# One VectorE instruction of 1024 columns in place of two of 512 in the running sum of the probabilities

## What is computed

```
q, k, v = (z @ w_qkv.T) split into 8 heads of 32
scores  = einsum("bhnd,bhmd->bhnm", q, k) / sqrt(32)
attn    = softmax(scores, axis=-1)
sa      = einsum("bhnm,bhmd->bhnd", attn, v)
out     = sa @ w_agg.T + b_agg
```

## Time and profile before

| | us |
|---|---|
| median of 3 executions | 1822.64 |
| lowest, highest | 1817.12, 1822.80 |
| span of the profiled execution | 1855.2 |
| PE busy | 1449.7 (78%) |
| DVE busy | 1112.1 (60%) |
| ACT busy | 883.7 (48%) |
| POOL busy | 575.7 (31%) |
| first exp of batch 0, last exp of batch 7 | 131.8, 1532.4 |

### The profile page before, as it was taken

The page is one execution under the profiler, slowest core; times in us unless marked ns, Lnnn a source line. Parts: engine busy times, 40 slices in busy tenths (PEclk is TensorE's granted clock), DMA queues, the critical chain, the costliest instruction groups (busy, mean ns, idle before and its releaser), DMA issues. The chain is left out here.

```text
span 1855.2 us, 28644 instructions
## 1 busy us (share of the span) xinstructions
PE 1449.7 (78%) x10308; PEld 902.9 (49%) x10308; DVE 1112.1 (60%) x2276; ACT 883.7 (48%) x1281; POOL 575.7 (31%) x1142
## 2 busy tenths in 40 slices
PE   5669998989698969996999699969998995213565
PEld 3435655555455536554655465536555554112444
DVE  3226765666476747564667476657665884764553
ACT  2235564656465636564656466646565772000111
POOL 1303410452035203520352035204520221035664
PEclk7788998999899989998999899989999997557777
DMA  2152015101610161005300630053004303012221
GB/s 73 36 120 63 1 40 134 56 1 37 143 51 1 29 144 58 1 6 141 85 1 1 138 92 1 1 127 102 2 1 108 99 2 98 0 44 81 90 89 60
DMA packets 73757, 109.47 MB, mean 59 GB/s; under 512 B 12410, under 2 KB 56443, under 8 KB 73595
## 3 DMA queue, kind: packets, MB, share of 16 engines
q1 hardware_dynamic: 66409, 90.47, 19.6%
q0 software_dynamic: 6144, 16.79, 2.8%
q10 hardware_dynamic: 1042, 0.01, 0.0%
HBM read 20.98 MB, written 25.43 MB: 25 GB/s over the span
## 5 line engine op out<-in xcount | busy, mean ns | idle before, releaser
L843 ACT ACTIVATE probs<-scores 128x1024 f32<-128x1024 f32 x512 | 519.3, 1023 | 265.0 <-PE scores L622 171.7
L622 PE MATMUL scores<-query_stack,key_stack 128*128 128x256 f32 x2048 | 410.5, 325 | 110.4 <-issue 86.0
L1062 DVE TENSOR_TENSOR prob_sum<-prob_sum,probs 128x512 f32<-128x512 f32 x640 | 454.8, 759 | 16.2 <-ACT probs L843 16.2
L622 PEld LDWEIGHTS scores<-query_stack,key_stack 128*128 128x128 f32 x2048 | 294.8, 196 | 256.8 <-issue 188.0
L640 PE MATMUL acc<-probs,v_sb 128*32 128x256 f32 x4096 | 331.0, 396 | 8.8 <-ACT probs L843 8.8
L862 POOL TENSOR_TENSOR attn_T<-acc_sb 128x256 f32<-128x256 f32 x64 | 61.9, 966 | 645.8 <-DVE acc_sb L1047 634.2
L663 PE MATMUL shared<-w_sb,chan 128*128 128x512 f32 (+1 forms) x512 | 188.6, 504 | 5.0 <-DVE chan L974 5.0
L1047 DVE RECIPROCAL acc_sb<-acc_sb 128x256 f32<-128x256 f32 x64 | 111.6, 1744 | 107.6 <-ACT acc_sb L833 107.6
L1182 PE MATMUL y_ps<-w_sb,zT 128*128 128x256 f32 x256 | 90.1, 488 | 76.8 <-DVE result L1341 51.4
L1351 ACT ACTIVATE zT<-zT_ps 128x256 f32<-128x256 f32 x64 | 24.6, 384 | 257.4 <-PE zT_ps L1173 209.3
L640 PEld LDWEIGHTS acc<-probs,v_sb 128*32 128x32 f32 x4096 | 88.4, 109 | 111.6 <-issue 43.0
(11 more groups left out here) (164 smaller groups left out, 2046.4 us busy)
## 6 DMA issues: line engine op xcount, KB each, us to landing
query_stack<-hi SPq DMA_DIRECT2D x128, 128.0 KB, 2.5
key_stack<-hi SPq DMA_DIRECT2D x128, 128.0 KB, 2.6
x_sb<-in_x_dram SPq DMA_DIRECT2D x8, 1024.0 KB, 8.2
key_stack<-lo SPq DMA_DIRECT2D x64, 128.0 KB, 2.5
query_stack<-lo SPq DMA_DIRECT2D x64, 128.0 KB, 2.5
v_sb<-v_next SPq DMA_DIRECT2D x16, 512.0 KB, 3.7
out_dram<-resid SPq DMA_DIRECT2D x16, 512.0 KB, 3.3
tokens_scratch<-resid SPq DMA_DIRECT2D x16, 512.0 KB, 4.2
```

Source lines behind the costliest of these rows:

```text
L622: last = pe.matmul(score_ps[u % 2][:, QB * r:QB * (r + 1)], key_stack[:, HG * g + r, P * kt:P * (kt + 1)], query_stack[:, HG * g + r, QB * ...
L843: act.activation(probs[:, u % 3, :], score_ps[u % 2][:, :], ACT.Exp, scale=DH ** -0.5) \
L1062: dve.tensor_tensor(total[:, part], probs[:, (u - 1) % 3, part] if kt == 1 else total[:, part], probs[:, u % 3, part], ALU.add).then_inc(s ...
```

## The change

The loop over the two halves goes. One `tensor_tensor` adds all 1024 columns, it counts the semaphore `summed` up by 1, and the three waits on that semaphore (of the next add, of TensorE's `total` and of ScalarE's exp) count adds and not halves. Nothing changes place.

```
-                    pe.wait_ge(s["summed"], 2 * added * (blk + 1))
+                    pe.wait_ge(s["summed"], added * (blk + 1))
...
-                        act.wait_ge(s["summed"], 2 * (added * ((u - 3) // T) + min(max((u - 3) % T, 1), added)))
+                        act.wait_ge(s["summed"], added * ((u - 3) // T) + min(max((u - 3) % T, 1), added))
...
-                for h in range(2):
-                    part = slice(BANK * h, BANK * (h + 1))
-                    if kt > 1:
-
-                        dve.wait_ge(s["summed"], 2 * (added * (u // T) + kt - 2) + h + 1)
-                    dve.tensor_tensor(total[:, part], probs[:, (u - 1) % 3, part] if kt == 1 else total[:, part],
-                                      probs[:, u % 3, part], ALU.add).then_inc(s["summed"], 1)
+                if kt > 1:
+
+                    dve.wait_ge(s["summed"], added * (u // T) + kt - 1)
+                dve.tensor_tensor(total, probs[:, (u - 1) % 3, :] if kt == 1 else total, probs[:, u % 3, :],
+                                  ALU.add).then_inc(s["summed"], 1)
```

## The result

The changed kernel takes 1864.8 us (median of 4 runs, 1864.3 to 1867.1) against 1822.7 us (4 runs, 1817.1 to 1831.9) for the kernel before: a ratio of 1.0218, with a 95% interval of 1.0191 to 1.0246. It is 42 us slower, 3 us above the upper end of the stated range (1816 to 1862) and 14 above the 1830 to 1851 that the forecast counted as its own. From the first to the last exp of each of the eight batches, added up, it went from 1295.8 to 1337.1 us, +41.3, which is nearly the whole result; the seven boundaries between batches have 104.8 and 106.0 us. Batch 2, by its exps, went from 170.5 to 177.8.

The account below looks back on a forecast made before the run. TensorE's queue was taken to bound the kernel nearly everywhere; changed waits (+15 us) and slow clock (+5) made +20 us on the profiled span, carried to the 1822.6 us median: 1843 us, range 1816 to 1862.

Parts of the forecast that it names:

- The instruction: VectorE's add: 1.21 us for 1024 columns; 0.07 us gained per add where another instruction follows freely, 0.04 lost between dependent adds.
- Rival 4: An add costs 1.37 us, more than its slope says: +0.8 x 7 = +6 us, within the forecast's range, no separate chance.
- GpSimd falls behind: Beside back-to-back adds, one GpSimd operation passes per VectorE instruction: once per 1.2 us with whole adds, per 0.6 with halves.
- Rival 1: GpSimd does not fall behind: the two +1.6 us go to zero, the gains stand, 1816 us; chance 0.17.
- Head scaling: TensorE's 3.4 us wait for GpSimd's head scaling grows by 1.6 us per loop batch, to 5.0; batch 0 by 1.07.
- Store chain: GpSimd chain ahead of the layer-norm rows (0.5 us TensorE wait at 534.4): ends later, +1.6 us in each of six batches.
- Rival 2: Only one of the two places with +1.6 us moves, the other has unseen slack: 1828 us; chance 0.20.
- Exp at 615.4: TensorE's 2.3 us wait for an exp behind a GpSimd chain that meets single adds: +0.2 us per loop batch.
- The gains: Shorter waits: line 922 -0.6 us, batch end -0.1, line 957 -0.07, an exp in batch 0 -0.6, batch 7 -0.8 net.
- The sum without the clock: All changes in waits: 15.6 us over six loop batches, +0.4 in batch 0, -0.8 in batch 7, together +15 us.
- The clock: TensorE at half clock after longer waits: 1.7 us lost at three of 13 places, +5 us; bounds -6 and +22.
- Rival 3: The clock falls behind every longer wait: 15 + 22 = +37 us, 1860 us; chance 0.13.

Follow-up runs that it names:

- the two filled kernels: Changed kernel and kernel before, each with idle 128x512 matmuls put ahead of TensorE's long waits: 1851.5 us (ratio 0.9984) and 1833.8 us (ratio 0.9901).

## Why the forecast was right in its mechanism and short in its sum

**What bounds the kernel.** Right. The time followed TensorE's waits and clock, and 56 us off VectorE's busy time (1112.1 to 1055.8) bought nothing.

**The instruction.** Right: an add that nothing holds up takes 1.22 us (the row at 537.19), forecast 1.21 (the terms as printed, 0.68 + 2 x 0.26, give 1.20), and two dependent ones span 2.49 to 2.50, which is twice that and a gap of 0.05 or 0.06, forecast 0.03. The mean of 1.255 us holds the hold-ups by GpSimd. Rival 4 (1.37) is out. The formula that the forecast took from the Trainium skill, "VectorE: DVE Perf Modes", gives 1.22 for it, and the trace agrees. The saving of 61 us that the same formula gave is close to the 59 of busy time, but by luck: as said above, most of the 59 is standing behind GpSimd that went away.

**GpSimd falls behind.** Right, and the term that decides. Rival 1 fell with the rows of 1.2 us on four columns. The rule of the Trainium skill that stood beside it ("SBUF — State Buffer", section "Who interferes with whom": the second to issue blocks until the first has finished) fits these rows, but not the two of 1.58 and 1.71 us, which sat through two halves and through four quarters. Head scaling: forecast 5.0 us, measured 5.0. Store chain: forecast an end at 534.99 to 535.27 and +1.6; measured a wait of 0.5 that became 2.2, +1.8. Rival 2 fell too: both places moved, and the run with halves at the head scaling alone shows them apart.

**Exp at 615.4.** Too small. Forecast +0.2, measured +0.7 (2.3 to 3.0). The picture was right, one long hold in place of two short ones at +0.2, but the chain meets three such adds and the forecast counted the price once; three times 0.2 is near what was measured. Over six batches this is 3 us of wait; what it did to the clock is the larger part, below.

**The gains.** Right: line 922 from 0.9 to 0.3, line 957 from 0.9 to 0.8, the batch's end down by 0.2 in sum, where 0.1 was forecast (two waits of 1.3 and 0.6 became 0.7 and 1.0), PE idle in batch 7 down by 0.9 where 0.8 was forecast.

**The sum without the clock.** Forecast +15, measured +16.3 of idle time in the traces and 17.7 between the two filled kernels. By part: the six loop batches 14.7 (forecast 15.6), batch 7 -0.9 (-0.8), batch 0 +2.5 (+0.4). Batch 0 has a wait for the transfer of x_sb that was 7.4 us instead of 4.5, and in the changed kernel's second profile 4.7, so it goes from run to run and not with the change. Without these 2.9 us the idle time grew by 13.4, a little under the forecast; the wait at the head scaling of batch 0 grew by 0.9 (forecast 1.07), and its 2.2 us for an exp shrank by 0.7 (0.6).

**The clock: the step that failed.** The forecast says "Three of 13 is near the two in six of the 2.3 us waits, since the 2.1 us ones are a little shorter: +5", with an upper bound of 22. Measured: 47.7 us more of slow time, 24 us lost. By place, half of the slow time that came on in the loop batches is 11.5 us behind the rows, 10.4 behind the exp and 2.1 behind the head scaling. Two things were wrong in it. The chance was read from two of six, at a wait of 2.3 us, and carried over to a wait at another place; the waits of 2.2 us at the rows were followed by 0.50 in six of six. And the list of places was too short: the exp's own wait, forecast as nearly unmoved, went to 3.0 us and from two slow stretches in six to six in six, and at the 5.0 us wait the stretch was 6.8 us in three of the six batches, at the 3.4 us wait of before in one. Rival 3 (1860 us) had the mechanism and was the nearest number; its bound of one stretch of 3.4 us per place, 22 us, is just under the 24 measured, since some stretches were 6.8 us. What decides between no stretch, one and a longer one isn't only the length of the wait: in before a wait of 2.3 us at the same place was followed by 0.56, 1.00 and 0.55 in batches 1, 2 and 3. What it is stays open.

**The carrying over.** The span of 1855.2 lay 33 us above the median, and the places were taken as the same in both. Right: the ratio was 1.0218 where the kernel before takes 1822.7 us, and 1.0229 where it takes 1855.0.

## What to carry to other kernels

An instruction count is the wrong thing to save where another engine has to wait for the instruction to end, as GpSimd did here (1.2 us for 0.20 us of work): ask of a long two-input VectorE instruction which GpSimd chain stands beside it and who waits for the chain's end; cut such instructions short there, and leave them whole elsewhere. Count a TensorE wait of the lengths seen here (2.2 to 5.0 us) twice, once for itself and once for the slow clock that may follow it (it did in six of six batches at three places of the changed kernel), and list for this every such wait that there will be after the change, not only those that the change moves. Where such a wait can't be removed, work put into it, in the end even idle work, gives the clock's part back (most of the 44 and 21 us here).

## What the runs showed that I had not expected

Filling waits with idle products made both kernels faster, by 44 and 21 us. Of the 44 us, the six loop batches have 36; 7 us more came at the boundaries between batches, where no product was added (104.5 us in seven of them became 97.5). It isn't the clock: PE idles 8 us less there (87.8 to 79.9), and its slow time is 9 and 11 us. Why it idles less is open.

The expert stage behind the last exp, which no kernel here touched, took 322.8 us in the profile of before and 292.0 in that of after (length, PE, PEld, DVE, ACT, POOL with their counts, granted clock, DMA share, GB/s):

```profile
1532.40:1855.20 322.80, 140.76 (x542) 105.83 (x534) 170.22 (x568) 33.30 (x82) 131.66 (x164) 0.67 0.21 66
```

```profile
1571.20:1863.20 292.00, 128.63 (x542) 98.76 (x534) 170.30 (x566) 33.30 (x82) 131.70 (x164) 0.67 0.23 73
```

The first is of before, the second of after. DVE, ACT and POOL are busy for the same time in both, and the mean granted clock is the same; PE is busy for 12 us more in the first; the bytes are the same too (66 GB/s over 322.8 us, 73 over 292.0). It isn't the kernel: before has 322.8 us in its first profile and 290 in its second, and the changed kernel 292.0 in its first and 321 in its second. All eight kernels run on one chip have 321 to 324, all three on the other 290 to 292, so it seems to go with the chip; only two chips are on record, and why is open. A profile from one chip must not be compared by its span with one from another.
